# Attention values placed by on-chip DMAs instead of TensorE products in a four-layer gated cross-attention kernel

## What is computed

```python
query = _split_heads(q @ w_q); key_ = _split_heads(k @ w_k); value = _split_heads(v @ w_v)
scores = jnp.einsum('bhqd,bhkd->bhqk', query, key_) / jnp.sqrt(D_K)
scores = jnp.where(mask == 0, -1e9, scores)
x = jnp.einsum('bhqk,bhkd->bhqd', jax.nn.softmax(scores, axis=-1), value)
```

## Time and profile before

| | us |
|---|---|
| three runs | 396.02, 396.36, 394.38 (median 396.02) |
| profiled execution | 393.49 |
| its span, first to last instruction | 391.7 |
| PE busy | 367.7 (94%) |
| DVE / ACT / POOL busy | 279.1 / 214.0 / 104.5 |
| mean granted TensorE clock | 0.991 |

### The profile page before, as it was taken

How to read it: one execution, slowest core, us unless ns; L and a number is a source line. 1 busy time by engine, 2 the same in 40 slices (tenths; PEclk the granted TensorE clock), 3 DMA queues, 4 the chain that set the end, 5 groups by cost and what they waited for, 6 DMA issues and landing times. The chain is left out here.

```text
span 391.7 us, 5900 instructions
## 1 busy us (share of the span) xinstructions
PE 367.7 (94%) x2150; PEld 277.2 (71%) x2150; DVE 279.1 (71%) x644; ACT 214.0 (55%) x392; POOL 104.5 (27%) x113
## 2 busy tenths in 40 slices
PE   7998899999999999998989999999989989899996
PEld 2576656867677888885668897767667746789765
DVE  5438675297868777778677777788777778887495
ACT  1312414337897988975246674466546533466382
POOL 4202060232125353622102211032556432100220
PEclk9999969999999999999999999999999999999999
DMA  6800000101036532200000100015452000000001
GB/s 190 344 2 1 2 0 2 54 3 54 0 112 220 156 84 79 82 2 0 2 0 5 50 29 0 2 28 165 161 154 89 2 0 2 0 3 2 0 2 54
DMA packets 13345, 20.88 MB, mean 53 GB/s; under 512 B 1787, under 2 KB 5397, under 8 KB 13317
## 3 DMA queue, kind: packets, MB, share of 16 engines
q1 hardware_dynamic: 12768, 20.02, 16.2%
q0 software_dynamic: 96, 0.32, 0.3%
q10 hardware_dynamic: 453, 0.18, 0.2%
HBM read 19.92 MB, written 0.59 MB: 52 GB/s over the span
## 5 line engine op out<-in xcount | busy, mean ns | idle before, releaser
L1194 DVE TENSOR_TENSOR rlo<-banks,rhi 128x512 fp32r<-128x512 f32 x64 | 44.0, 690 | 20.9 <-ACT rhi L721 20.1
L1397 PE MATMUL banks<-heat 128*128 128x512 bf16 x174 | 49.5, 401 | 2.9 <-POOL heat L414 2.9
L1390 PE MATMUL banks<-hhi,wuh 128*128 128x512 f32 x128 | 51.5, 402 | 0.0
L737 ACT ACTIVATE banks<-banks,b1s 128x512 f32<-128x512 f32 x64 | 42.4, 662 | 15.4 <-PE banks L1392 15.0
L438 POOL TENSOR_TENSOR rstd<-var,neghalf 128x4 f32<-128x4 f32 x16 | 16.5, 1032 | 127.1 <-DVE var L888 127.1
L1392 PE MATMUL banks<-hhi,wul 128*128 128x512 f32 x128 | 50.0, 391 | 0.0
L1391 PE MATMUL banks<-hlo,wuh 128*128 128x512 f32 x128 | 49.9, 390 | 0.0
L1390 PE MATMUL banks<-rhi,wdh 128*128 128x512 f32 x96 | 40.2, 419 | 8.8 <-DVE rlo L1194 3.8
L463 POOL TENSOR_TENSOR wul<-up_raw,wuh 128x512 fp32r<-128x512 f32 x16 | 21.1, 1321 | 66.0 <-ACT wuh L615 66.0
L1749 PEld LDWEIGHTS banks<-vals,shared 128*128 128x128 f32 x320 | 37.4, 191 | 0.7 <-ACT shared L796 0.6
L1749 PE MATMUL banks<-vals,shared 128*128 128x27 f32 (+1 forms) x320 | 37.6, 270 | 0.1
(11 more groups left out here) (271 smaller groups left out, 729.2 us busy)
## 6 DMA issues: line engine op xcount, KB each, us to landing
rowB<-rowd SPq DMA_DIRECT2D x32, 256.0 KB, 4.7
up_raw<-in_w SPq DMA_DIRECT2D x8, 258.0 KB, 4.5
down_raw<-in_w SPq DMA_DIRECT2D x8, 256.0 KB, 5.4
up_raw<-in_v SPq DMA_DIRECT2D x8, 256.0 KB, 2.8
down_raw<-in_v SPq DMA_DIRECT2D x8, 128.0 KB, 3.3
const<-in_const SPq DMA_DIRECT2D x1, 911.0 KB, 7.2
mats<-in_mats SPq DMA_DIRECT2D x1, 640.0 KB, 5.4
mats<-in_mats SPq DMA_DIRECT2D x1, 576.0 KB, 4.1
```

The source lines that it names most:

```text
L737: nc.scalar.activation(bank[BANKS1[g % 4]][:, :], bank[BANKS1[g % 4]][:, :], ACT.Gelu, bias=b1s[p][:, c_:c_ + 1]).then_inc(q["gelu"], 1)
L1194: V.tensor_tensor(rlo[g % 4][:, :], bank[BANKS1[g % 4]][:, :], rhi[g % 4][:, :].bitcast(F32), ALU.subtract).then_inc(q["lo"], 1)
L1390: mm(o, lh, rh, start=start, stop=False)
L1397: mm(o[:, :], heat[:, 0:P], heat[:, :], start=True, stop=True)
```

## The change

The products `replicate`, the copies `replicated` and the maskings `mask_values` go. SP copies each head's values from `vN` straight to their place in `vals` by DMA (`place_values`), and the zeros come from one memset of all of `vals` at the start. A head's 77 rows can cross a chunk's border of 128 partitions, so 16 heads make 25 pieces (`VALUE_PIECES`), each a DMA of 1 to 77 partitions x 2 batches x 8 floats. `vals` becomes one array over layers and batches, `kT` and `vN` get a copy for each layer, and the matrix `rep` leaves the constants. Where the products stood, filler products stand. In `scores_of`, the mask products of the first tile move ahead of its wait for the queries.

```diff
-K_REP = K_LT4 + 16
-K_PAIR = K_REP + CH * P
+K_PAIR = K_LT4 + 16
...
 SP:
+            def place_values(n):
+                sp.wait_ge(kv["act"], n + 1)
+                for j in range(H):
+                    for c_ in range(j * K // P, ((j + 1) * K - 1) // P + 1):
+                        r0, r1 = max(j * K, c_ * P), min((j + 1) * K, (c_ + 1) * P)
+                        o = ((CH - 1 - c_) * HW + j - FIRST[c_]) * VW
+                        sp.dma_start(vals[r0 - c_ * P:r1 - c_ * P, n, :, o:o + DH],
+                                     vN[n][r0 - j * K:r1 - j * K, :, j * DH:(j + 1) * DH]).then_inc(kv[f"bd{n}"], 16)
+            sp.wait_ge(kv["one"], 1)
+            place_values(0)
             for p in range(2):
                 sp.wait_ge(q["dl"], p + 1)
...
                 for j in range(4):
                     next_row(0, 4 * i + j)
+                if i == 1:
+                    place_values(1)
...
 POOL:
-            for n in range(2):
-                for b in range(B):
-                    nc.gpsimd.memset(vals[n][b][:, CH * HW * VW:], 0.0)
+            nc.gpsimd.memset(vals[:, :, :, :], 0.0)
...
+            for n in range(2):
+                for b in range(B):
+                    one = vals[:, n, b, 0:CH * HW * VW].rearrange("p (c h e) -> p c h e", h=HW, e=VW)[:, :, :, DH]
+                    last = nc.gpsimd.tensor_scalar(one, pair, 1.0, 0.0, ALU.mult, ALU.add)
+            last.then_inc(kv["one"], 1)
             pool.wait_ge(kv["act"], 1)
-            mask_values(0, 0)
...
-            mask_values(0, 1)
...
 ACT:
-            replicated(0, 0)
...
-            replicated(0, 1)
...
-                replicated(1, n)
...
 PE:
             pe.wait_ge(l1["rt"], B)
-            replicate(0, 0)
-            keep_busy(bank[0], 5)
+            keep_busy(bank[5], 8)
+            pe.wait_ge(kv["act"], 1)
             for b in range(B):
                 transposes(4 + b)
                 keep_busy(bank[4 * b + 2], 2)
-                pe.wait_ge(kv["reps"], 1)
...
             keep_busy(bank[6], 4)
-            replicate(0, 1)
+            keep_busy(bank[2], 4)
...
             keep_busy(bank[6], 4)
-            pe.wait_ge(kv["reps"], 2)
             pe.wait_ge(ld["moe1"], 32)
...
-                    pe.wait_ge(at["qT"], 2 * n + b + 1)
+                    if u > 0:
+                        pe.wait_ge(at["qT"], 2 * n + b + 1)
...
-                    if u % NT == 0:
-                        pe.wait_ge(kv["bd"], 2 * n + b + 1)
+                    if u == 0:
+                        pe.wait_ge(kv[f"bd{n}"], 16 * VALUE_PIECES)
...
                 scores_of(0)
-                replicate(1, n)
+                keep_busy(bank[5], 8)
```

More of the change, by code:

```diff
@@ L48 @@
 VW = DH + 1
+VALUE_PIECES = sum(((j + 1) * K - 1) // P - j * K // P + 1 for j in range(H))
 MASKED = -1e30
@@ L119, in flamingo_program @@
         head_in_group = const[:, K_HEAD:K_HEAD + HG]
-        def rep(c):
-            return const[0:K, K_REP + c * P:K_REP + (c + 1) * P]
         pair = const[:, K_PAIR:K_PAIR + CH * HW].rearrange("p (c h) -> p c h", h=HW)
@@ L203, in flamingo_program @@
         nb = sb("nb", [P, B, NT, K], BF16)
-        kT = sb("kT", [P, B * K])
+        kT = [sb(f"kT{n}", [P, B * K]) for n in range(2)]
         kbg = [sb(f"kbg{b}", [P, HG, K]) for b in range(B)]
@@ L207, in flamingo_program @@
         table = sb("table", [P, 1])
-        vN = sb("vN", [K, B, D])
-        vals = [[sb(f"vals{n}_{b}", [P, (CH * HW + H - HW) * VW]) for b in range(B)] for n in range(2)]
-        vbd = [[v[:, 0:CH * HW * VW].rearrange("p (c h e) -> p c h e", h=HW, e=VW) for v in pair_] for pair_ in vals]
+        vN = [sb(f"vN{n}", [K, B, D]) for n in range(2)]
+        vals = sb("vals", [P, 2, B, (CH * HW + H - HW) * VW])
         Sx = [sb(f"Sx{i}", [P, CH * P]) for i in range(2)]
@@ L246, in flamingo_program @@
              ["g", "u", "silu", "mul", "hi", "lo", "free", "uh", "ul", "dh", "dl", "ys", "mult", "add"]}
-        kv = {n: sem(f"kv_{n}") for n in ["pe", "act", "pool", "rep", "reps", "bd"]}
+        kv = {n: sem(f"kv_{n}") for n in ["pe", "act", "pool", "one", "bd0", "bd1"]}
         at = {n: sem(f"at_{n}") for n in
@@ L289, in flamingo_program @@
         BANKR = [bank[6], SIDE]
-        BANKV = {(0, 0): 5, (0, 1): 2, (1, 0): 5, (1, 1): 5}
         MULT = {"q": list(range(GROUPS_)), "r": [0, 1, 4, 5, 2, 6, 3] + list(range(7, GROUPS_))}
@@ L318, in _ @@
                 sp.dma_start(x[b][:, :, :], a["x"][b].rearrange("(t p) d -> p t d", p=P)).then_inc(ld[f"x{b}"], 16)
-            sp.dma_start(const[:, 0:K_REP], a["const"][:, 0:K_REP]).then_inc(ld["ident"], 16)
+            sp.dma_start(const[:, 0:K_PAIR], a["const"][:, 0:K_PAIR]).then_inc(ld["ident"], 16)
             sp.dma_start(mats[:, 0:M0, :], a["mats"][:, 0:M0, :]).then_inc(ld["l0"], 16)
@@ L325, in _ @@
             sp.dma_start(mats[:, M2:, :], a["mats"][:, M2:, :]).then_inc(ld["l3"], 16)
-            sp.dma_start(const[:, K_REP:], a["const"][:, K_REP:]).then_inc(ld["const"], 16)
+            sp.dma_start(const[:, K_PAIR:], a["const"][:, K_PAIR:]).then_inc(ld["const"], 16)
             sp.dma_start(rwT[:, :], a["rwT"]).then_inc(ld["moe1"], 16)
@@ L445, in add_bias, with key @@
                                         ALU.add).then_inc(x_biased, 1)
-            def key(b):
-                nc.gpsimd.tensor_tensor(kbg[b][:, :, :], kT[:, b * K:(b + 1) * K].unsqueeze(1).broadcast_to([P, HG, K]),
+            def key(n, b):
+                nc.gpsimd.tensor_tensor(kbg[b][:, :, :], kT[n][:, b * K:(b + 1) * K].unsqueeze(1).broadcast_to([P, HG, K]),
                                         head_in_group.unsqueeze(2).broadcast_to([P, HG, K]),
                                         ALU.mult).then_inc(kv["pool"], 1)
[L453 to L458, removed]
             def split_up(i, p, sems):
@@ L489, in _ @@
             pool.wait_ge(ld["const"], 16)
+            for n in range(2):
[3 more added lines that the diff above has]
+            last.then_inc(kv["one"], 1)
             pool.wait_ge(kv["act"], 1)
             for b in range(B):
-                nc.gpsimd.tensor_scalar(vbd[0][b][:, :, :, DH], pair, 1.0, 0.0, ALU.mult, ALU.add)
-                key(b)
-            mask_values(0, 0)
-            for b in range(B):
-                nc.gpsimd.tensor_scalar(vbd[1][b][:, :, :, DH], pair, 1.0, 0.0, ALU.mult, ALU.add)
+                key(0, b)
             pool.wait_ge(ld["l3"], 16)
@@ L528, in _ @@
             norm(9)
-            mask_values(1, 0)
             for p in range(2):
@@ L561, in _ @@
                 if 1 <= i <= B:
-                    key(i - 1)
+                    key(1, i - 1)
             norm(13)
@@ L565, in _ @@
                 add_bias(1, b)
-            mask_values(1, 1)
             norm(14)
@@ L590, in values @@
                 bk, bv = ((0, 4), (4, 6))[n]
[L591 to L602, removed]
+                nc.scalar.activation(kT[n][:, :], bank[bk][:, 0:B * K], ACT.Copy, scale=float(DH) ** -0.5)
+                nc.scalar.activation(vN[n][:, :, :], bank[bv][0:K, 0:B * D], ACT.Copy).then_inc(kv["act"], 1)
             def up_hi(i, p, mixture, chunks, sems, in_psum):
@@ L1423, in context @@
                 last.then_inc(kv["pe"], 1)
[L1425 to L1432, removed]
             pe.wait_ge(heat_ready, 1)
@@ L1713, in scores_of @@
                            nb[:, b, t, :].unsqueeze(1).broadcast_to([P, HG, K]), start=True, stop=False)
-                    if u >= 1:
+                    if u == 0:
+                        pe.wait_ge(at["qT"], 2 * n + b + 1)
+                    else:
                         pe.wait_ge(at["sub"], NG * T)
@@ L1749, in values_of @@
                         last = mm(bank[0][:, h0 * VW:(h0 + heads) * VW], tile(PT[T % 2], c_),
-                                  vals[n][b][:, r0:r0 + heads * VW], start=(c_ == 0), stop=(c_ == CH - 1))
+                                  vals[:, n, b, r0:r0 + heads * VW], start=(c_ == 0), stop=(c_ == CH - 1))
                     last.then_inc(at["O"], 1)
@@ L1924, in shape_constants @@
     pairs = np.arange(SPAN)
-    c[pairs % K, K_REP + pairs] = 1
     pair = np.zeros((P, CH, HW), np.float32)
```

## The result

The change makes the kernel 4.0% slower: four runs of it have a median of 410.94 us (409.66 to 412.73), four of before 395.2 (394.1 to 396.36), ratio 1.0401, 95% interval 1.0344 to 1.0459. The forecast was 406.7 (395.1 + 11.6) with a range of 399.5 to 414.

What follows compares the result with a forecast made beforehand. PE, busy 94% of 391.7 us, was taken as the bound. A loss of 15.6 us less gains of 3.0, 0.8 and 0.2 gave +11.6 on 395.1, so 406.7 us, range 399.5 to 414.

Steps and rivals of the forecast that it cites:

- What a piece costs: SP, second 25 pieces ahead of expert 6: 0.48 to 0.73 us each, taken as 0.69, 17.2 us in all.
- The slack: Expert 6 lands 3.2 us before ACT wants it, plus 0.3 between DVE and PE; PE stops 13.7 us.
- The start after a stop: PE starts slow after the long wait for expert 6: 1.9 us lost, range 0 to 1.9.
- Place one: First removed products, near 51 us: with fillers PE is on time for h's transposes; gain 3.0 us, range 1.0 to 3.0.
- Place two: Second removed products, near 79 to 84 us: PE reaches h's transposes earlier; gain 0.8 us, range 0.2 to 0.8.
- Places three and four: Removed products near 193 and 328 us: nothing at the third, covered by DVE; 0.2 us gained at the fourth.
- At nothing: No cost or gain from ACT's copies, POOL's maskings, larger memset, smaller constant load and the first 25 pieces.
- Data as the pace: Rival: pieces' data on the fullest DMA engine delays expert 6; 411 to 424 us, chance 0.17 shared with dearer pieces.
- Quick pieces: Rival: pieces issue in under 0.14 us, so PE never stops for expert 6; 391.1 us, chance 0.08.
- Gains that don't come: Rival: the clock falls at 51 us as before; forecast 2 us higher, 408.7, inside the range, no separate chance.
- paced by the issue: Main case: expert 6 late by SP's issue time for the second 25 pieces; 399.6 to 410.2 us, chance 0.68.
- dearer pieces: Rival: each piece costs more than assumed; 411 to 424 us, chance 0.17 shared with pacing by data.

Runs made afterwards that it cites:

- experiment 1: Changed kernel with layer 3's 25 pieces issued behind the first mixture's last expert loads: 390.8 us, ratio 0.9919 to the kernel before.
- experiment 2: Kernel before plus 25 DMAs of the same shapes on SP ahead of expert 6, copying values to an unread scratch tile: 412.11 us, ratio 1.0473.
- experiment 3: Changed kernel with 12 of layer 3's 25 pieces left in place and 13 behind the last expert loads: median 402.17 us, ratio 1.0133 from two runs.
- experiment 4: Changed kernel, pieces in place but cut to 16, 48 or 64 rows, layer 2's to one batch: 406.22 us, ratio 1.0337 to the kernel before.
- Experiment 7: Experiment 1's kernel with ten unread products and five fillers replacing the eight fillers before the first transposes: 394.68 us, ratio 1.0022 to the kernel before.
- experiment 6: Two kernels: the one before minus five fillers before the first transposes, 393.79 us, ratio 1.0003; experiment 1's minus eight there, 392.57 us, ratio 0.9973.

## Why the prediction was right, and where its sizes were off

**Sign and cause.** Expert 6 behind the pieces, ACT waiting for it, PE full and so unable to make it up: experiments 1 and 2 show that this is the loss, all of it as far as their intervals can tell.

**What a piece costs.** The step "I take `ctxN`'s, whose shape it is: 25 x 0.69 = 17.2" was too low: 0.81 and a gap of 0.05, 21.5 us. Both upper bounds (0.64, 0.68) came from loads; the range's end of 18.2 didn't hold the term.

**The slack.** 3.2 + 0.3 us were taken; 5.3 were there on ACT's side (21.45 - 16.13), 5.6 on PE's. Two of these are in the landing: expert 6's second DMA lands 3.2 us after issue, not 5.3. In the kernel before it was issued half a microsecond behind row loads of 256 KB; that these slowed it is argued, not tried. So PE stopped 15.8 us where 13.7 was forecast: an issue time 4.3 us too low and a slack 2.1 us too small, of which one hid half of the other by luck.

**The start after a stop.** 1.9 us taken, as the most, 2.4 measured. It doesn't follow the length of the stop: the half clock lasts 5.7 us behind 5.4 us of waiting (experiment 3), 3.2 behind 12.0 (experiment 4), 4.9 behind 15.4 (experiment 2) and 5.3 behind 15.8. Loss in all: 15.8 + 2.4 = 18.2, forecast 15.6; experiment 2 says 18.4.

**Place one.** 3.0 forecast, 3.4 measured between the two profiles; against experiment 2's profile, which has the former order there and 10.4 us in place of 11.8, it is 1.9. So the size differs between executions. The mechanism held in both halves (late PE and fallen clock). The step "POOL does about as much beside it as before, so I leave it" was wrong: h of the second batch takes 1.11 us, not 1.88. POOL now makes the copies of ones beside it and the `key` products after it; that these made h slow before is argued, not tried.

**Place two.** 0.8 forecast, 0.3 measured. PE's router products were early, but the mixture's first product waits for DVE's next operation, and beside POOL's split that one took 1.64 us (L1080), where before it took 0.69 beside the same split. In the changed kernel POOL's split had begun 0.18 us ahead of it; in the former one it began 0.12 us behind, and there the split was the longer one (1.70 us and not 1.26).

**Places three and four.** Three: nothing, as forecast. Four: 0.2 forecast; the second scores came 0.5 us earlier (4.29 us behind the first, 343.71 to 348.00, and not 4.81, 324.60 to 329.41), but nothing of it is left at the end of the span, which comes 67.2 us behind the first scores and came 67.1 us behind them before. In the changed kernel's profile the clock was at 0.66 from 353 to 358 us, in the other it stayed at 1.00, so one pair of profiles can't tell what place four is worth.

**At nothing.** This held: the first 25 pieces took 21.2 us and moved expert 2's issue to 79.6 us, and no engine but ACT at expert 6 waited for an expert's load; the larger memset took 1.41 us. Experiment 7, in which ACT's copies and POOL's maskings stay out, gains nothing.

**The rivals.** Data as the pace: the loads of experts 6 and 7 landed in 3.1 to 4.0 us behind all 25 pieces, so no backlog. Quick pieces: the shortest took 0.63 us. Gains that don't come: the clock did fall at place one in the profile of experiment 3, where the change's own PE order stands, so this rival is true of some executions. The measured 410.94 us lies just above 410.2, the end of the case that had 0.68 (paced by the issue, at 0.48 to 0.73 a piece): the mechanism is that case's, the size is that of "dearer pieces", which had a part of 0.17.

**The sum.** 18.4 - 3.2 (experiment 1's 0.8%) = +15.2 us; measured 15.7; forecast 11.6.

## What to carry to other kernels

A queue that only issues DMAs is a program like any other: find the load behind the insertion, its reader, and how long that load was early; more than that is paid in full where the reader is on a full engine's chain. Price a DMA by issue time times count in its own shape, and put the batch where its queue is idle, as experiment 1 did. Rows that 16 divides were cheaper to issue, but the kernels that showed it left values out: 77 rows can't be cut so without more pieces, and whether that pays was not tried. A late engine and its clock are two causes of one delay: taking out the fillers alone, or the short products and the fillers both, gained nothing that can be told from zero; putting fillers in the place of the short products gained 0.8%.

## What the runs showed of the hardware that was not expected

The granted clock also fell at a place where no kernel changed PE's program. The windows (PE alone) of the changed kernel's and, second, of the former kernel's profile from 16 us:

```profile
16.00:18.00 2.00, 2.00 (x8) 0.50 0.76 280
18.00:20.00 2.00, 2.00 (x9) 0.72 0.01 2
```

```profile
16.00:18.00 2.00, 1.96 (x10) 1.00 1.05 376
```

The first twenty fillers took 7.42 us in the one and 6.23 in the other, so the start at half speed also differs in length. Together this put the changed kernel's profile 2.6 us behind at 47 us. The same fall stands in two of the experiments' profiles (of the twelve early pieces, clock 0.83 from 14 to 24 us, and of the second kernel of experiment 6) and in none of the others. In the three profiles that have it, `context(0)` begins at 50.1 to 50.2 us, in the seven others at 47.2 to 48.3. All three are of kernels that hold the change, of which four more profiles are without the fall; there were three profiles of kernels with the former order, all without. Whether the change's larger memset or smaller constant load has a part in it is not shown. A difference of 1 to 3 us between two single profiles of such a kernel says nothing before that stretch has been taken off.
